# Expert layers of a hybrid network: token rows gathered by an inverted order, and up weights held stationary

## The reference, cut to what matters

```python
# m = 4096 tokens, H = 128, F = 256, E = 8 experts, TOP_K = 2
probs = softmax(x @ gate_w)
top_w, top_i = top_k(probs, 2)
top_w = top_w / sum(top_w)
route = zeros((m, E)); route[token, top_i] = top_w
out = 0
for e in range(E):
    h = silu(x @ w1[e]) * (x @ w3[e])
    out = out + route[:, e:e+1] * (h @ w2[e])
```

## Time and profile before

| what | value |
|---|---|
| median of three runs | 1973.47 us (1968.79 to 1974.69) |
| the profiled execution | 1971.24 us, its span 1969.5 us |
| busy share of the span | PE 67%, DVE 77%, ACT 47%, POOL 13% |
| mean granted clock of PE | 0.828 |
| expert layer 1, from its first instruction to the last scatter | 862.2 to about 1084 us |
| expert layer 2 | 1742.9 us to the end |

### The profile page before, as it was taken

How to read it: one execution, slowest core, us unless ns; L and a number is a source line. 1 busy time by engine, 2 the same in 40 slices (tenths; PEclk the granted TensorE clock), 3 DMA queues, 4 the chain that set the end, 5 groups by cost and what they waited for, 6 DMA issues and landing times. The chain is left out here.

```text
span 1969.5 us, 42398 instructions
## 1 busy us (share of the span) xinstructions
PE 1324.6 (67%) x15088; PEld 718.6 (36%) x15088; DVE 1517.7 (77%) x2925; ACT 918.3 (47%) x2025; POOL 253.8 (13%) x298
## 2 busy tenths in 40 slices
PE   4689999999999999941999580000000188822998
PEld 2215555554555555340666250000000033421665
DVE  5698999899989998071665676999999799971665
ACT  4508888888888888950443560002222100030443
POOL 6000000000000000025045000000000000034044
PEclk9859999999999999975999675555555599965999
DMA  3611111111111100032243229311212100012243
GB/s 90 175 42 27 32 30 30 30 30 30 42 45 30 30 3 3 2 111 58 53 68 50 79 104 161 111 43 43 57 46 60 54 0 0 0 52 58 56 67 44
DMA packets 118652, 100.85 MB, mean 51 GB/s; under 512 B 23665, under 2 KB 100018, under 8 KB 118066
## 3 DMA queue, kind: packets, MB, share of 16 engines
q1 hardware_dynamic: 101570, 84.79, 16.8%
q0 software_dynamic: 11264, 8.92, 3.1%
q10 hardware_dynamic: 5616, 4.47, 1.4%
HBM read 55.98 MB, written 31.21 MB: 44 GB/s over the span
## 5 line engine op out<-in xcount | busy, mean ns | idle before, releaser
L727 DVE TENSOR_REDUCE att_negmax<-att_ps_max 128x1 f32<-128x1024 f32 x512 | 620.9, 1223 | 66.0 <-PE att_ps_max L590 37.3
L715 ACT ACTIVATE att_probs<-att_ps_prob 128x512 f32<-128x512 f32 x1024 | 556.3, 595 | 128.7 <-PE att_ps_prob L605 126.5
L590 PE MATMUL att_ps_max<-av_k_op,av_q_op 81*32 81x512 bf16 x4096 | 417.9, 401 | 13.2 <-PEq L104 7.2
L605 PE MATMUL att_ps_prob<-av_q_op,av_k_op 99*32 99x512 bf16 x4096 | 407.2, 382 | 2.7
L625 PE MATMUL att_ps_acc<-att_probs,att_vq 128*32 128x256 f32 x4096 | 313.4, 379 | 0.0
L1935 PE MATMUL out_ps_y<-all_bo_row,all_ones 1*128 1x128 f32 x2 | 0.8, 481 | 373.2 <-PEq L104 373.2
L590 PEld LDWEIGHTS att_ps_max<-av_k_op,av_q_op 81*32 81x32 bf16 x4096 | 111.9, 97 | 146.5 <-DVE att_negmax L727 44.9
L605 PEld LDWEIGHTS att_ps_prob<-av_q_op,av_k_op 99*32 99x32 bf16 x4096 | 108.7, 95 | 146.1 <-ACT att_probs L715 94.3
L625 PEld LDWEIGHTS att_ps_acc<-att_probs,att_vq 128*32 128x32 f32 x4096 | 130.3, 111 | 78.4 <-issue 0.5
L1154 ACT ACTIVATE moe_moe_gate<-moe_moe_ps_h 128x256 f32<-128x256 f32 x122 | 46.8, 383 | 214.4 <-PE moe_moe_ps_h L1095 201.3
L1935 PEld LDWEIGHTS out_ps_y<-all_bo_row,all_ones 1*128 1x128 f32 x2 | 0.5, 308 | 373.4 <-issue 373.4
(11 more groups left out here) (277 smaller groups left out, 2038.1 us busy)
## 6 DMA issues: line engine op xcount, KB each, us to landing
moe_moe_xin<-expert_rows SPq DMA_DIRECT2D x182, 72.0 KB
av_k_op<-terms_k SPq DMA_DIRECT2D x48, 216.0 KB
av_q_op<-terms_q SPq DMA_DIRECT2D x144, 72.0 KB
solve_dec_and_windows<-solve_Xw SPq DMA_DIRECT2D x16, 256.0 KB, 3.0
solve_dec_and_windows<-solve_k SPq DMA_DIRECT2D x16, 256.0 KB, 3.7
terms_q<-qkv_parts_q SPq DMA_DIRECT2D x8, 384.0 KB, 2.6
terms_k<-qkv_parts_k SPq DMA_DIRECT2D x8, 384.0 KB, 3.1
all_w_all<-in_f_w SPq DMA_DIRECT2D x24, 128.0 KB, 2.5
```

Source lines behind the costliest of these rows:

```text
L590: mm = pe.matmul(ps_max[c * STRIP:(c + 1) * STRIP, a % 2, k * CH:(k + 1) * CH], q_op[s][0:R_ALL, h, at:at + STRIP], k_op[s][0:R_ALL, h, k ...
L605: mm = pe.matmul(ps_prob[c * STRIP:(c + 1) * STRIP, j % 2, :], k_op[s][0:R_END, h, at:at + STRIP], q_op[s][0:R_END, h, half * CH:(half + 1 ...
L715: act.activation(probs[:, j % PROBS, :], ps_prob[:, j % 2, :], ACT.Exp).then_inc(s_exp, 1)
L727: dve.tensor_reduce(negmax[:, s % 2, a:a + 1], ps_max[:, a % 2, :], AX.X, ALU.max, negate=True).then_inc(s_maxed, 1)
```

## The change

Rows are no longer scattered. ACT's normalised rows go to DRAM in token order, in four transfers by SP. The sorted order is inverted: DVE writes for every token a one-hot row of its place within the sorted tile (`low_hot`) and a row with the tile and token number (`named`), and PE adds up 32 products of the two, which gives `ids`, the token at every sorted place. POOL gathers the 32 sorted tiles by `ids` into `xs`, which stay in SBUF with their weights. Each is turned once into `xgT`, now of all 32 tiles, and a pass addresses its tile there with a register (`row_of`), so PE reads two numbers for each pass. The list of passes is computed on 128 partitions, one per tile, and put in order by 16 small products; it is on one partition only.

In a pass ACT copies the expert's w1 and w3 to a buffer of three (`copy_weights`, with a read on ACT), and `up` takes the copy as stationary in four blocks of 128 columns and the tile as moving, so that its result has F on the partitions. ACT's Silu and DVE's product then give `hT` itself; `turn_h` and `take_h` go. The expert's weight is no longer in the product: `add` multiplies by it, and addresses it by a second number that DVE reads (`c_at`). `down` is two passes behind `up` instead of three.

The diff, cut to its core (the tables that POOL writes, 36 small memsets of `incid` among them, the names of tiles and semaphores, and the rest of the removed `plan` are left out; of DVE's new functions the new lines alone are shown):

```diff
-    sp.wait_ge(s_scat, landed)
-    for n in range(2):
-        sp.dma_start(xin[:, n, :], scr.xg[0:P, :]).then_inc(s_load[n], 16)
-    sp.wait_ge(s_plan, 1)
-    for n in range(2, NPASS):
-        if n >= NXIN:
-            pair = (n - NXIN) // 2
-            sp.wait_ge(s_gturn, pair + 1)
-            sp.wait_ge(s_mine, pair + 1)
-        row = sp.value_load(row_at[0:1, n:n + 1], min_val=0, max_val=(NT - 1) * P)
-        sp.dma_start(xin[:, n % NXIN, :], scr.xg[bass.ds(row, P), :]).then_inc(s_load[n % NXIN], 16)
-        if n == NXIN - 1:
-            sp.dma_start(ids[:, :, :], scr.xg.bitcast(mybir.dt.uint32)[:, COL_ID:COL_ID + 2].rearrange(
-                "(t p) o -> p t o", p=P)).then_inc(s_rid, 16)
+    sp.wait_ge(s_pad, 1)
+    sp.wait_ge(s_weight, 1)
+    for q in range(0, NPIECE, 2):
+        some = slice(q * PIECE, (q + 2) * PIECE)
+        sp.wait_ge(s_xn, q + 2)
+        sp.dma_start(scr.xg.rearrange("(t p) o -> p t o", p=P)[:, some, :], xr[:, some, :]).then_inc(s_rows, 16)
...
-    pool.wait_ge(s_ids, 2)
-    pool.wait_ge(s_xn, NPIECE)
-    pool.wait_ge(s_weight, 1)
-    pool.wait_ge(s_slot, 1)
+    pool.wait_ge(s_rows, 16 * NPIECE // 2)
+    pool.wait_ge(s_ids, 1)
     for t in range(NT):
-        pool.indirect_dma_start(scr.xg, bass.IndirectOffsetOnAxis(slot[:, t:t + 1], 0), xr[:, t, :],
-                                None).then_inc(s_scat, 16)
+        if t >= NSEM:
+            pool.wait_ge(s_load[t % NSEM], 16 * (gathered + t // NSEM))
+        pool.indirect_dma_start(xs[:, t, :], None, scr.xg,
+                                bass.IndirectOffsetOnAxis(ids[:, t:t + 1], 0)).then_inc(s_load[t % NSEM], 16)
...
-    pe.wait_ge(s_code, 1)
-    pe.matmul(spread_ps, g.ones[:, :], spread[:, :, :].rearrange("p i n -> p (i n)"), start=True,
-              stop=True).then_inc(s_spread, 1)
+    pe.wait_ge(s_count, 1)
+    pe.matmul(ps_prefix, earlier[:, :], local[:, E - 1:E], start=True, stop=True).then_inc(s_prefix, 1)
+    pe.wait_ge(s_turns, 1)
+    pe.wait_ge(s_tables, 13)
+    for e in range(E):
+        pe.matmul(ps_row, tile_b[:, :], turn_of[:, e, :], start=(e == 0), stop=(e == E - 1))
+    for e in range(E):
+        mm = pe.matmul(ps_exp, exp_b[:, e:e + 1], turn_of[:, e, :], start=(e == 0), stop=(e == E - 1))
+    mm.then_inc(s_passes, 1)
+    pe.wait_ge(s_lanes, 1)
+    pe.wait_ge(s_named, 1)
+    for t in range(NT):
+        if t % ONES_AT == 0:
+            pe.wait_ge(s_low, t // ONES_AT + 1)
+        mm = pe.matmul(ps_i[:, 0:2 * NT], low_hot[:, t, :], named[:, t, :], start=(t == 0), stop=(t == NT - 1))
+    mm.then_inc(s_inv, 1)
...
     def turn_rows(j):
+        pe.wait_ge(s_load[j % NSEM], 16 * (gathered + j // NSEM + 1))
         wait_used(pe, s_gT, j)
-        for n in range(2 * j, min(2 * j + 2, NPASS)):
-            pe.wait_ge(s_load[n % NXIN], 16 * (n // NXIN + 1))
-            mm = pe.transpose(ps_g[:, (n % 2) * P:(n % 2 + 1) * P], xin[:, n % NXIN, 0:P], g.ident[:, :])
-        mm.then_inc(s_gturn, 1)
-
-    def up(n, at0):
-        pe.wait_ge(s_gT, n // 2 + 1)
+        pe.transpose(ps_g[:, j % 4 * P:(j % 4 + 1) * P], xs[:, j, 0:P], g.ident[:, :]).then_inc(s_gturn, 1)
+
+    def up(n, row):
+        pe.wait_ge(s_gT, min(n // 2 + 1, NT))
+        pe.wait_ge(s_wb, n + 1)
         wait_used(pe, s_h, n - 2)
-        cols = slice((n % 2) * P, (n % 2 + 1) * P)
-        pe.matmul(ps_up[n % 3][:, :, :].rearrange("p w f -> p (w f)"), xgT[:, n // 2 % 3, cols],
-                  wall[:, bass.ds(at0, 2 * F)], start=True, stop=True).then_inc(s_up, 1)
-
-    def turn_h(n):
+        for i in range(2 * MF):
+            mm = pe.matmul(ps_up[n % 3][:, i * P:(i + 1) * P], wbuf[:, n % 3, i * P:(i + 1) * P],
+                           xgT[:, bass.ds(row, P)], start=True, stop=True)
+        mm.then_inc(s_up, 1)
+
+    def down(n, at0):
         pe.wait_ge(s_h, n + 1)
-        wait_used(pe, s_hT, n - 1)
-        for i in range(MF):
-            mm = pe.transpose(ps_ht[n % 2][:, i * P:(i + 1) * P], hs[:, n % 3, i * P:(i + 1) * P],
-                              g.ident[:, :])
-        mm.then_inc(s_hturn, 1)
-
-    def down(n, at0):
-        pe.wait_ge(s_hT, n + 1)
         wait_used(pe, s_sum, n - 1)
         for i in range(MF):
             mm = pe.matmul(ps_y[n % 2][:, 0:P], hT[:, n % 3, i * P:(i + 1) * P],
@@ -1113,25 +1139,26 @@
 
     pe.wait_ge(g.s_experts, 16 * 3 * E)
     pe.wait_ge(s_plan, 1)
+
+    def row_of(n):
+        return pe.value_load(row_at[0:1, n:n + 1], min_val=0, max_val=(NT - 1) * P)
+
     def start_of(n):
         return pe.value_load(w_at[0:1, n:n + 1], min_val=0, max_val=(E - 1) * WE)
 
+    row, starts = row_of(0), {0: start_of(0)}
     turn_rows(0)
-    starts = {0: start_of(0)}
+    turn_rows(1)
     for n in range(NPASS):
-        up(n, starts[n])
+        up(n, row)
         if n + 1 < NPASS:
-            starts[n + 1] = start_of(n + 1)
+            row, starts[n + 1] = row_of(n + 1), start_of(n + 1)
         if n >= 2:
-            turn_h(n - 2)
-        if n % 2 == 0 and n + 2 < NPASS:
-            turn_rows(n // 2 + 1)
-        if n >= 3:
-            down(n - 3, starts.pop(n - 3))
+            down(n - 2, starts.pop(n - 2))
+        if n % 2 == 0 and n // 2 + 2 < NT:
+            turn_rows(n // 2 + 2)
     for n in (NPASS - 2, NPASS - 1):
-        turn_h(n)
-        down(n - 1, starts.pop(n - 1))
-    down(NPASS - 1, starts.pop(NPASS - 1))
+        down(n, starts.pop(n))
 
 @block.scalar
 def _(act):
@@ -1148,35 +1175,46 @@
             act.wait_ge(s_gap, 1)
             act.activation(tanh[:, :, :], gap[:, :, :], ACT.Tanh, scale=0.5).then_inc(s_tanh, 1)
 
+    act.wait_ge(s_tables, 11)
+    act.wait_ge(s_high, 1)
+    act.activation(named[:, :, 0:NT], high_hot[:, :, :], ACT.Copy, scale=lane[:, 0:1]).then_inc(s_lanes, 1)
+
+    def copy_weights(n, at0):
+        act.activation(wbuf[:, n % 3, :], wall[:, bass.ds(at0, 2 * F)], ACT.Copy).then_inc(s_wb, 1)
+
+    def start_of(n):
+        return act.value_load(w_at[0:1, n:n + 1], min_val=0, max_val=(E - 1) * WE)
+
     def silu(n):
         act.wait_ge(s_up, n + 1)
         wait_used(act, s_h, n - 2)
-        act.activation(gate[:, n % 3, :], ps_up[n % 3][:, 0, :], ACT.Silu).then_inc(s_silu, 1)
-
-    def take_h(n):
-        act.wait_ge(s_hturn, n + 1)
-        wait_used(act, s_y, n - 2)
-        act.activation(hT[:, n % 3, :], ps_ht[n % 2][:, 0:MF * P], ACT.Copy).then_inc(s_hT, 1)
-
+        act.activation(gate[:, n % 3, :], ps_up[n % 3][:, 0:F], ACT.Silu).then_inc(s_silu, 1)
+
+    act.wait_ge(g.s_experts, 16 * 3 * E)
+    act.wait_ge(s_plan, 1)
+    for n in range(3):
+        copy_weights(n, start_of(n))
     for n in range(NPASS):
+        if n + 3 < NPASS:
+            at0 = start_of(n + 3)
         silu(n)
-        if n >= 2:
-            take_h(n - 2)
-    for n in (NPASS - 2, NPASS - 1):
-        take_h(n)
+        if n + 3 < NPASS:
+            copy_weights(n + 3, at0)
 
...
+    def experts_of_tiles():
+        dve.wait_ge(s_tables, 4)
+        also(dve.tensor_scalar(upper[:, :], ends[:, :], tile_to[:, 0:1], None, ALU.min))
+        chain.done(dve.tensor_scalar(lower[:, :], base[:, :], tile_from[:, 0:1], None, ALU.max))
+        chain.done(dve.tensor_tensor(meets[:, :], upper[:, :], lower[:, :], ALU.is_gt))
+        dve.wait_ge(s_incid, 1 + E - 1 + PAIRS)
+        chain.done(dve.tensor_tensor(hits[:, :, :], incid[:, :, :],
+                                     meets[:, :].unsqueeze(1).to_broadcast([P, E, PAIRS]), ALU.mult))
+        chain.done(dve.tensor_reduce(needed[:, :], hits[:, :, :], AX.X, ALU.max))
+        dve.tensor_tensor_scan(local[:, :], unit[:, 0:E], needed[:, :], 0.0, ALU.mult,
+                               ALU.add).then_inc(s_count, 1)
+
+    def places():
+        dve.wait_ge(s_carry, 2)
...
+
+    def order_passes():
+        dve.wait_ge(s_prefix, 1)
+        chain.done(dve.tensor_copy(prefix[:, :], ps_prefix))
+        dve.wait_ge(s_count, 1)
+        chain.done(dve.scalar_tensor_tensor(out=upto[:, :], in0=local[:, :], scalar=prefix[:, 0:1],
+                                            in1=needed[:, :], op0=ALU.add, op1=ALU.mult))
+        dve.wait_ge(s_tables, 5)
+        dve.tensor_tensor(turn_of[:, :, :], order[:, :].unsqueeze(1).to_broadcast([P, E, P]),
+                          upto[:, :].unsqueeze(2).to_broadcast([P, E, P]), ALU.is_equal).then_inc(s_turns, 1)
+
+    def invert():
+        dve.wait_ge(s_tables, 11)
+        chain.done(dve.tensor_tensor(above[:, :, :], slot_f[:, :].unsqueeze(2).to_broadcast([P, NT, NT + 1]),
+                                     steps[:, :].unsqueeze(1).to_broadcast([P, NT, NT + 1]), ALU.is_gt))
+        dve.tensor_tensor(high_hot[:, :, :], above[:, :, 0:NT], above[:, :, 1:NT + 1],
+                          ALU.subtract).then_inc(s_high, 1)
+        chain.done(dve.tensor_reduce(full[:, :], above[:, :, 0:NT], AX.X, ALU.add))
+        chain.done(dve.scalar_tensor_tensor(out=low[:, :], in0=full[:, :], scalar=-float(P), in1=slot_f[:, :],
```

(64 more changed lines are left out.)

219 lines of the change are left out of this document (107 added, 112 removed).

## The result

The changed kernel takes 2038.82 us (median of 4 runs, 2037.18 to 2040.43) against 1972.95 for the kernel before: a ratio of 1.0337, 95% interval 1.0318 to 1.0356. The forecast was 1982, a loss of 0.4%; it is 3.3%. That lies inside the stated range (1948 to 2042), but only just, and by luck: the top of the range was set for an address in each product or a falling clock, and neither is what happened. The profiled execution took 2037.85 (span 2036.1).

A forecast was written before the change was run, and what follows sets the result against it. Bounds: when the first pass starts and a pass's array time, with PE's queue taking the array's place. Per layer +30.3 - 28.4 + 1.0 + 1.3 = +4.2, +8.4 for two, giving 1982 us; range 1948 to 2042.

The forecast's parts named there:

- Array work 1.39 us: In a pass after the change: up 0.90, down 0.45 and fewer row turns make 1.39 us of array time.
- PE's queue 1.97 us, +30.3 us a layer: In the passes: PE's issuing with two reads takes 1.97 us, replaces the array as bound, and adds 30.3 us a layer.
- the 1.3 of the cold start: First passes: the array starts at half clock, about two passes at 2.78 us, adding 1.3 us a layer.
- this sign of the prediction: In the passes: PE's idle put down to DVE, ACT or a gather instead of issue would show the forecast wrong.
- VectorE 1.6 to 1.7 next: In the passes: DVE's queue with two reads takes 1.6 to 1.7 us, hidden under 1.97, but the next bound.
- Start -28.4: Start of the passes: first up at 1781.0 instead of 1809.4 us, saving 28.4 us a layer.
- Tail +1.0: End of the passes: the last three adds wait for two reads each, adding 1.0 us a layer.
- Clock 1.00: In the passes: PE's granted clock stays at 1.00 although the array works 70% of a pass.
- only the first two gathers lie on the path, the other 30 (1.27 us each) run beside passes: Start of the passes: POOL's other 30 gathers were given no cost, since passes need a tile each 3.9 us.
- More issuing: Rival on PE's queue: one more semaphore instruction in up gives 2002 us, an address for each product 2040; chance 0.12.
- The clock falls: Rival on PE's clock in the passes: half the time at half clock gives 2043 us, all of it 2128; chance 0.10.
- The reads hide: Rival on PE's reads overlapping: DVE's queue bounds at 1.68 us a pass, 1930 us, or the array, 1875; chance 0.12.

The follow-up runs named there:

- e8: e7, but VectorE reads one packed number a pass and works out row and column in registers, instead of reading two; 1868.52 us, ratio 0.9483.
- e1: The changed kernel, but from the fifth on each gather waits for one more pass's up products, so about one in 2 us; 1973.41 us, ratio 1.0007.
- e2: The changed kernel, but TensorE waits for all 32 gathers before it turns the first rows; 2052.53 us, ratio 1.0411.
- e3: The changed kernel, but SyncE loads the 32 tiles by plain transfers in token order, in place of POOL's gathers; 1969.15 us, ratio 0.9986.
- e7: e1, but ScalarE copies the down weights too (six buffers), so TensorE reads only the row of a pass; 1911.20 us, ratio 0.9701.
- e4: The kernel before, with 32 unused indirect gathers of the sorted rows added, issued by POOL after the first up product; 2053.18 us, ratio 1.0412.

## Why the prediction was wrong

**Step by step.** *Array work 1.39 us:* e8 shows 1.40 with an array that never rests. *PE's queue 1.97 us, +30.3 us a layer:* in e1, e2 and e3, where nothing else disturbs, the passes take 179.0 to 179.2 us, 31.6 more than before: the 30.3 forecast and the 1.3 of the cold start. That it is the queue and not the round of waits is shown by e7: one read less on TensorE takes 0.38 us off a pass. In the steady passes the queue's steps follow each other within 0.11 us through a whole pass (1963.67 to 1965.59), also where the profile puts the array's idle time down to VectorE's add, so this sign of the prediction was badly chosen. So was the one for VectorE: its idle time before an add is put down to `down` (1.03 us at 2021.14), not to issue. The four products share an address, as taken from the earlier trace rows. *VectorE 1.6 to 1.7 next:* e7, 1.61. *Start -28.4:* -29.7. *Tail +1.0:* the last adds are 1.46 and 1.45 us apart as forecast, the last y scatter starts 5.73 us after the last `up` instead of 5.11, +0.6. *Clock 1.00:* in the steady passes, yes. Without the stall a layer is then +31.6 - 29.7 + 0.6 = +2.5 where +4.2 was forecast, +5.0 for two where +8.4 was. e1's profiled execution is 3.1 us longer than that of the kernel before, its median 0.8; the rest of the 5.0 lies in parts outside these sums, which were not taken apart.

**The step that failed** is in the start of the passes: "only the first two gathers lie on the path, the other 30 (1.27 us each) run beside passes". The gathers were costed by who waits for their rows, and no one does. What was not asked is what their stream does to engines that do not wait for it. It cost 32.7 us a layer (e1 against the changed kernel), and this one missing term is 65.4 us in two layers where the forecast was 57 low; the other terms came out some 8 us cheaper than forecast and hid the rest. The trace before could not price it: its 32 scatters, the nearest row, ran while TensorE was silent, and its indirect transfers beside passes, those of y, start some 3 to 4 us apart. It was a cover taken at nothing without a row that shows both at once; e4 puts the two together in the old kernel and pays 80 us.

**The rivals.** "More issuing", with an address for each product, had 2040 as its time and is not what happened: one address for eight records. "The clock falls" had 2043 for half the time; the clock is 0.59 in the stall, but e1 has the same passes and is at 1.00, so it fell because TensorE had nothing to do. "The reads hide" is refuted as a rival, but its numbers come near once the reads are taken away: 1930 and 1875 forecast, 1911 (a pass of 1.61 us where it had 1.68) and 1868.5 measured.

**What is open.** The late reports came in every run with whole rows moved by indirect transfers 1.26 us apart beside the passes with all their reads. In the changed kernel they were gone at 2.0 or 2.9 us apart and with plain transfers of the same bytes, and in groups of eight they cleared after each; in the kernel before they came with rows of 288 bytes or more, in either direction; and the changed kernel with one read less on TensorE or on VectorE did not have them. The cause stays open: no run shows what the stream and the passes share, nor what the reads have to do with it. In layer 2 the first late report is that of `up(1)`, at 1817.12 for products that ended at 1814.84, and the reads of VectorE's first `add` start at 1838.88, so the traffic of those reads did not begin it. A place in memory or a time in the program that the edit shifts would fit, but no run singled one out. One rival stands untested: every execution timed here has a traced span and granted clock, so each was recorded while it ran, and TensorE's steps stand 0.69 us apart in that record during the stall. Whether the recording takes part in it, and so whether the stall is there without it, was not measured. The Trainium skill (DMA: Bandwidth & Descriptors, Latency and other measured facts) guesses, for another matter (two of the sixteen DMA engines are usually slower), that the descriptor rings of POOL's transfers crowd some ports of the memory; no run here shows it, nor that it would touch TensorE.
